# A gated delta-rule layer on one core: taps moved to ScalarE and GpSimd, 2 KB transfer rows, and a new order on every engine

## What is computed

```python
def attn(h):                       # h = layernorm(x)
    q, k, v, z = split(h @ w_qkvz.T)          # 32 heads of 64
    b, a = split(h @ w_ba.T)
    q, k, v = conv4(q), conv4(k), conv4(v)    # causal, 4 taps, each channel by itself
    g, beta = -exp(A_log) * softplus(a + dt_bias), sigmoid(b)
    q, k = l2norm(q) * 64 ** -0.5, l2norm(k)
    for t in range(256):                      # per head
        S = S * exp(g[t])
        S = S + outer(k[t], (v[t] - k[t] @ S) * beta[t])
        o[t] = q[t] @ S
    return rmsnorm(o) * norm_weight * sigmoid(z) @ w_out.T
x = x + layernorm(attn(layernorm(x)))
x = x + layernorm((silu(gate) * up) @ w_down.T)   # gate, up from layernorm(x) @ w_gate_up.T
```

## Time and profile before

| | us |
|---|---|
| median of 3 runs | 3099.59 |
| range of these | 3080.13 to 3100.36 |
| the profiled execution | 3095.35 |
| its span in the trace | 3093.5 |

### The profile page before, as it was taken

How to read it: one execution, slowest core, us unless ns; L and a number is a source line. 1 busy time by engine, 2 the same in 40 slices (tenths; PEclk the granted TensorE clock), 3 DMA queues, 4 the chain that set the end, 5 groups by cost and what they waited for, 6 DMA issues and landing times. The chain is left out here.

```text
span 3093.5 us, 101425 instructions
## 1 busy us (share of the span) xinstructions
PE 2889.1 (93%) x42816; PEld 1953.0 (63%) x42816; DVE 2445.7 (79%) x5610; ACT 1752.3 (57%) x3242; POOL 1103.3 (36%) x904
## 2 busy tenths in 40 slices
PE   6699999999999999999999999999999999789998
PEld 3366666666666666666666666666666666655555
DVE  7688888888888888888888888888888888656554
ACT  6456666566556666666566566656666566424332
POOL 1444344444444444343444444444343344100000
PEclk9899999999999999999999999999999999899999
DMA  5454545554545555554455555544455445300000
GB/s 154 79 82 84 89 80 83 83 98 81 81 81 97 80 81 84 93 83 80 81 98 84 82 80 99 83 76 83 75 100 81 80 81 84 83 21 21 27 14 21
DMA packets 1298099, 241.85 MB, mean 78 GB/s; under 512 B 1248240, under 2 KB 1269104, under 8 KB 1296496
## 3 DMA queue, kind: packets, MB, share of 16 engines
q1 hardware_dynamic: 1297648, 235.36, 44.2%
HBM read 120.13 MB, written 39.58 MB: 52 GB/s over the span
## 5 line engine op out<-in xcount | busy, mean ns | idle before, releaser
L1342 PE MATMUL bank<-xT,w_sb 128*128 128x512 f32 x2048 | 982.1, 613 | 10.0 <-PEq L516 5.2
L784 POOL TENSOR_TENSOR kq<-kq,product 128x510 f32<-128x510 f32 (+2 forms) x384 | 448.9, 1182 | 723.4 <-ACT kq L873 713.4
L1342 PEld LDWEIGHTS bank<-xT,w_sb 128*128 128x128 f32 x2048 | 372.3, 191 | 374.4 <-issue 346.1
L772 POOL TENSOR_TENSOR dec_ap<-gcrow,gcb 128x1024 f32<-128x1024 f32 x64 | 121.8, 1902 | 657.2 <-DMA gcb<-gcb_d 657.2
L1088 DVE SCALAR_TENSOR_TENSOR kq<-bank,cw,kq 128x510 f32<-128x510 f32 (+2 forms) x384 | 285.7, 744 | 58.8 <-ACT kq L873 49.5
L1088 DVE SCALAR_TENSOR_TENSOR v_c<-bank,cw,v_c 128x510 f32<-128x510 f32 (+2 forms) x384 | 285.8, 744 | 15.9 <-ACT v_c L873 6.9
L1353 PE MATMUL bank<-kq 64*64 64x128 f32 x4096 | 276.7, 273 | 20.4 <-POOL kq L784 8.3
L940 ACT COPY delta<-bank 128x256 f32<-128x256 f32 x256 | 95.2, 372 | 341.8 <-PE bank L1410 341.5
L1457 PE MATMUL bank<-wo,u_sq 128*128 128x256 f32 x1024 | 261.0, 399 | 4.0 <-DVE u_sq L1180 3.5
L879 ACT ACTIVATE product<-bank,cw 128x512 f32<-128x512 f32 x384 | 249.1, 684 | 6.8 <-PE bank L1342 2.8
L1435 PE MATMUL bank<-ap_mat,delta 64*64 64x64 f32 x4096 | 243.0, 219 | 3.2 <-issue 3.1
(11 more groups left out here) (168 smaller groups left out, 5459.4 us busy)
## 6 DMA issues: line engine op xcount, KB each, us to landing
xT<-xT_d SPq DMA_DIRECT2D x64, 512.0 KB, 3.9
gcrow<-gcrow_d SPq DMA_DIRECT2D x128, 256.0 KB, 4.6
k_r<-k_tok SPq DMA_DIRECT2D x512, 64.0 KB, 2.3
v_r<-k_tok SPq DMA_DIRECT2D x512, 64.0 KB
a_d<-ap_mat SPq DMA_DIRECT2D x256, 64.0 KB
z_t<-z_d SPq DMA_DIRECT2D x256, 64.0 KB, 2.5
w_sb<-in_w_qkvz SPq DMA_DIRECT2D x8, 1024.0 KB, 6.8
x_un<-eye_un SPq DMA_DIRECT2D x64, 128.0 KB, 4.0
```

The lines of the kernel that those rows point to most:

```text
L784: nc.gpsimd.tensor_tensor(t[:, :, d:SEQ], t[:, :, d:SEQ], prod[:, :, 0:SEQ - d], ALU.add).then_inc(tap_added[i], 1)
L1342: ins = nc.tensor.matmul(bank[:, :], w_two[m.grp % 2][:, h, s * P:(s + 1) * P], xT[:, h, :], start=(h == 0), stop=(h == HT - 1))
```

## The change

It has three parts.

The first: the three further taps of v's second pair of heads (projection 5) become three ScalarE products and three GpSimd sums, as for q. `add_tap(m, 2, d)` adds into v_c. `TAPPED` gives the projection for each of the three.

The second: k_tok, v_r and k_r are laid out by halves of a row. The first half of all 16 groups comes first, then the second half (`by_half`), so a row of a `turned` transfer is 16 x 32 elements in one piece, 2 KB. `turn_v`, `turn_k`, `scale_k`, `scale_v`, `squares`, `residual` and `solve(0)` read or write through this layout.

The third: every engine's list in `turn` has a new order, with other waits and other bank places. The work per step is the same. TensorE's list now handles steps s[0] to s[4].

```diff
+            TAPPED = (2, 3, 5)
+
+            def by_half(t):
+
+                return t[:, :, :].rearrange("p g c -> p (g c)").rearrange("p (f g c) -> p f g c", f=2, c=W2)
+
+            def over_halves(t):
+
+                return t.rearrange("p (o g x) -> p o g x", o=1, x=1).broadcast_to([P, 2, G, W2])
...
-                                    sp.dma_start(dst[r:r + W2, :, W2 * f:W2 * f + W2], k_tok[q:q + W2, :, W2 * t:W2 * t + W2]) \
+                                    sp.dma_start(by_half(dst)[r:r + W2, f, :, :], by_half(k_tok)[q:q + W2, t, :, :]) \
...
-                        t = half_of(m, 1)[:, a, :].rearrange("p (s t) -> p s t", t=SEQ)
+                        t = (half_of(m, 1)[:, a, :] if a < 2 else v_c[:, 1, :]).rearrange("p (s t) -> p s t", t=SEQ)
...
-                        i, w = (TAPS - 1) * a + d - 1, (2 + a) * TAPS + TAPS - 1 - d
+                        i, w = (TAPS - 1) * a + d - 1, TAPPED[a] * TAPS + TAPS - 1 - d
...
-                        ins = nc.vector.transpose(k_tok[:, a * GP:(a + 1) * GP, :].rearrange("p g c -> p (g c)"), v_c[:, a, :])
+                        ins = nc.vector.transpose(by_half(k_tok)[:, :, a * GP:(a + 1) * GP, :], v_c[:, a, :].rearrange("p (g f c) -> p f g c", f=2, c=W2))
...
-                        nc.vector.tensor_tensor(kt[m.par][:, :, :], k_r[:, :, :], col(e_tail).broadcast_to([P, G, C]), ALU.mult).then_inc(kt_done, 1)
+                        nc.vector.tensor_tensor(kt[m.par][:, :, :].rearrange("p g (f c) -> p f g c", f=2), by_half(k_r), over_halves(e_tail), ALU.mult).then_inc(kt_done, 1)
```

SyncE's list, in which the transfers at the end of a turn change places:

```diff
-                            wait_for(sp, zt_done, s[5], 1)
-                            z_out(s[5])
-                            x_out(s[5])
-                            wait_for(sp, z_d_out, s[5], 16)
-                            z_back(s[5])
-                            wait_for(sp, x_d_out, s[5], 16)
-                            x_back(s[5])
-                        if s[3]:
-                            wait_for(sp, proj_full[4], s[3], 1, back=1)
-                            load_x(s[3])
                         if s[4]:
-                            identity_in(s[4])
+                            wait_for(sp, sub_done[14], s[4], 1)
+                            x_out(s[4])
+                            wait_for(sp, zt_done, s[4], 1)
+                            z_out(s[4])
+                            wait_for(sp, z_d_out, s[4], 16)
+                            z_back(s[4])
+                        if s[2]:
+                            wait_for(sp, proj_full[6], s[2], 1, back=1)
+                            load_x(s[2])
+                        if s[3]:
+                            wait_for(sp, x_d_out, s[3], 16, back=1)
+                            identity_in(s[3])
+                        if s[4]:
+                            wait_for(sp, x_d_out, s[4], 16)
+                            x_back(s[4])
```

More of the change, by code:

```diff
@@ new lines, in turn @@
+                        if s[2]:
+                            wait_for(dve, z16_done, s[2], 1)
+                            turn_back(s[2])
+                        if s[1]:
+                            wait_for(dve, tap_added[8], s[1], 1)
+                            turn_v(s[1], 1)
+                        if s[3]:
+                            wait_for(dve, var_log[1], s[3], 1)
+                            combine(s[3], 1, ring(s[3], 2))
+                        if s[1]:
+                            scale_k(s[1])
@@ L1560, in turn @@
-                        if s[3]:
-                            wait_for(pe, zoff_done, s[3], 1)
-                            solve(s[3], 0)
+                        if s[3]:
+                            wait_for(pe, delta_done[0], s[3], 1)
+                            advance(s[3], 0)
+                        if s[1]:
+                            project(s[1], 4, ring(s[1], 1))
+                        if s[3]:
+                            wait_for(pe, og_done[0], s[3], 1, back=1)
+                            output(s[3], 0)
+                            wait_for(pe, state_done[0], s[3], 1)
+                            key_state(s[3], 1)
@@ new lines, in turn @@
+                        if s[4]:
+                            wait_for(pe, z_exp[1], s[4], 1, back=-3)
+                            wait_for(pe, og_done[0], s[4], 1)
+                            project_out(s[4], 1, ring(s[4], 0))
+                        if s[3]:
+                            wait_for(pe, rhs_done[1], s[3], 1)
+                            solve(s[3], 1)
+                        if s[4]:
+                            project_out(s[4], 0, ring(s[4], 2))
+                        if s[3]:
+                            wait_for(pe, delta_done[1], s[3], 1)
+                            advance(s[3], 1)
+                            output(s[3], 1)
+                            wait_for(pe, state_done[1], s[3], 1)
+                            key_state(s[3], 2)
@@ new lines, in turn @@
+                        if s[1]:
+                            wait_for(pe, tap_prod[3], s[1], 1)
+                            project(s[1], 5, ring(s[1], 3))
+                        if s[3]:
+                            wait_for(pe, rhs_done[2], s[3], 1)
+                            solve(s[3], 2)
+                        if s[1]:
+                            wait_for(pe, tap_added[2], s[1], 1)
+                            scores(s[1], 0, ring(s[1], 2))
+                        if s[3]:
+                            wait_for(pe, delta_done[2], s[3], 1)
+                            advance(s[3], 2)
+                            output(s[3], 2)
+                            wait_for(pe, state_done[2], s[3], 1)
+                            key_state(s[3], 3)
@@ new lines, in turn @@
+                        if s[1]:
+                            project(s[1], 6, ring(s[1], 0))
+                        if s[3]:
+                            wait_for(pe, rhs_done[3], s[3], 1)
+                            solve(s[3], 3)
+                        if s[1]:
+                            wait_for(pe, tap_added[5], s[1], 1)
+                            wait_for(pe, tap_prod[8], s[1], 1)
+                            scores(s[1], 2, ring(s[1], 3))
+                        if s[3]:
+                            wait_for(pe, delta_done[3], s[3], 1)
+                            output(s[3], 3)
```

667 lines of the change are left out of this document (308 added, 359 removed).

## The result

The changed kernel took 3065.48 us, median of 7 runs (3060.48 to 3074.76), beside 3087.17 for the kernel before: ratio 0.992 with a 95% interval of 0.989 to 0.995. The forecast was 3034, a gain of 65 us; 22 came. Run twice more, each time on another chip, the same kernel gave 1.000 (0.998 to 1.002) and 1.000 (0.998 to 1.002). So the change is worth between nothing and 22 us.

A forecast was written before the change was run, and what follows sets the result against it. The matrix engine, busy 479.27 of 500 us, was taken as the bound, its idle as all there was to win. Terms -55 - 32 - 7 - 12 + 31 + 10 = -65 gave 3030 us profiled, 3034 beside the median, range 2992 to 3108.

The forecast's parts named there:

- PE's work itself is only put in another order.: Matrix engine, steady part: the reordering leaves its work as is; all the change can win lies in 1.67 us idle per turn.
- Group weights, +10 (0 to 14): Before join16_outer: next group's weights load ahead of identity_in and x_back, delaying x_row up to 2 us, 7 times: +10 us.
- Lower clock, -12: Behind the matrix engine's pauses: half of the 0.4 us per turn lost at 1.2 GHz comes back, -12 us (0 to -25).
- Pauses, -55: Runs of small matmuls: projections put between them let instruction blocks land, cutting 0.98 us idle per turn to 0.1, -55 us.
- the third rival: Matrix engine's pauses aren't the supply of instructions, so 55 and 12 us stay: 3101 us, chance 0.10.
- key_state 1, -32: Before key_state 1: project 4 between advance 0 and output 0 covers the wait for the state copy, 0.52 us per turn.
- z_t, -7: Before join16_inner: projections 5 and 6 ahead give z_t time to land, 0.17 to 0.05 us per turn, -7 us.
- New couplings, +31: Matrix engine's waits for VectorE before project 3, ScalarE before delta_out 0, and residual 1 before solve 1: 0.5 us per turn.
- ScalarE's chain (b): From the end of join_inner to delta_out 0: ScalarE needs 7.3 us against 7.1 of cover, late by 0.2.
- Taps 0, rows 0: VectorE's three fused tap operations saved, and 2 KB instead of 128 B transfer rows for k and v, each counted 0.
- rival 4: Moving the taps does nothing: the 2.2 us of VectorE are counted at zero; part of the forecast, no chance of its own.
- Rival 1: Pauses go but waits come in their place, 0.5 us becoming 1.5 per turn: +62, 3096 us, chance 0.15.

The follow-up runs named there:

- the weights late: Changed kernel with the next group's weights issued behind x_back instead of ahead of x_row and x_back: 3047.02 us (0.9898), then 3052.89 (0.9918) and 3057.20 (0.9933).
- the small program: Separate program without the computation, only large and small matmuls grouped, alternating or alone, with or without transfers: 2.21 us per pair and block grouped, 2.53 alternating.
- the second profile: The changed kernel, unaltered, run again on a second chip: 3076.13 us, ratio 1.0004.
- the later profile of before: The kernel before, unaltered, profiled again on another chip: 3071.96 us, 1.64 us idle a turn.
- the third of the changed kernel: The changed kernel, unaltered, run a third time on another chip: 3080.15 us, ratio 1.0000.
- a split project_out: Changed kernel with two extra 64-row matmuls in the middle of each project_out: 3100.90 us (1.0074); with them ahead of it instead, 3083.61 (1.0014).

## Why the prediction was wrong

The direction of the first comparison was right and its time lies in the range (2992 to 3108), but two thirds of the gain didn't come.

- *"PE's work itself is only put in another order."* This sentence failed. It sets the order's own price at zero; it is 0.67 us a turn, 41 us (0.82 without the 0.15 of wait that the shortest turn of before holds). Three more runs of 128-row matmuls make it, at some 0.3 us each. The trace of before had it already: 5.35 from start to start for three projections in one run, and 1.91 at 1539.80 for one alone.
- *Group weights, +10 (0 to 14).* Mis-sized: some 27 by undoing it. The place was right and even the sign of failure ("seven long waits before join16_outer of more than 2 us"); the waits are 2.6 each, and the clock behind each was not counted.
- *Lower clock, -12.* It gave back nothing: 27 slow projection matmuls before, 24 after (17 against 11 and 14 on other chips), since seven new long waits replaced the pauses as its main cause: of nine places with slow ones in the changed kernel six stand behind them. With the weights late 0 to 4 are left, so the step would have come.
- *Pauses, -55.* Without the seven waits for x_row the issue rows fell from 64 to 13 us, on later chips from 53 to 14: -52 and -39. The mechanism stands: the small program shows pauses at every 256th instruction and none where large matmuls stand between. So the third rival is out. By the Trainium skill (Runtime: NRT & Kernel Launch, "Instruction fetch mechanics") the cost of a block boundary is mostly hidden. In the small program that holds only with 128-row matmuls among the instructions: without them TensorE stops for 0.58 us in the mean.
- *key_state 1, -32.* 31.1 to 0.2 us, on later chips 38.8 to none. Right, and in full.
- *z_t, -7.* 10.5 to 0 and 7.4 to 0. Right.
- *New couplings, +31.* 18 us, on later chips 28: 10 to 11 for conv's result and residuals, and 8 to 17 for the state ahead of key_state 3, which the list of couplings doesn't have, though the new order takes its cover away (20.5 in the second profile). Of ScalarE's chain (b) nothing was seen. The size is near, the places are only in part.
- *Taps 0, rows 0.* The rows are 0. The taps are 0 only in a sum of separate terms: taken back in the new order they cost 40 to 58 us. The order could not stand without them. Whether the move does nothing in the old order, as rival 4 has it, was not tried.
- *Rivals.* Rival 1 came nearest by its time (3096 against 3065 to 3080), but not by its mechanism; VectorE was late for project 3 by 9.4 us in all, not by 149.

In the first pair the terms give: idle (-52 - 31 - 10 + 10 + 8 + 18) = -57, busy time +41 (0.66 a turn), together -16, against -20.6 for the two profiled executions. For the later profile of before and the third of the changed kernel, which are of two chips, idle is -39 - 39 - 7 + 11 + 17 + 17 = -40, and busy time +42 against it is nothing, as the ratio of 1.000.

## What to carry to other kernels

When waits are traded for cover by spreading large matmuls among small ones, count the runs: each separate one costs a fixed time (0.3 us here) on the engine that is the bound, and is worth it only where the hand-over that it covers is longer. Moving a covering block uncovers what it covered; look first for what stood on both sides of it. And see which instruction waits before a line of waits is called a remainder: the wait for the state went from one key_state and came up at another. Check where a rare large transfer stands in its queue: seven of them cost as much here as half the pauses. And a gain under one per cent wants more than one chip before it is believed.

## What the hardware showed that was not expected

- Changing between 64-row and 128-row matmuls costs TensorE some 0.3 us for the two changes of a run: 0.1 going in and 0.2 coming out in the kernels, 0.35 at a split project_out, 0.3 in the small program.
- TensorE stops for 0.25 to 0.94 us at each 256th instruction of small matmuls even with idle DMA engines, and not at all with 1.9 us of large matmuls ahead of each 256. I had taken the pause for 1.2 to 1.6 us.
- A bare wait can cost more than itself: behind 1.28 us of wait in a turn the granted clock was 0.50 for 5 us, three projections taking 8.14 in place of 5.42 us.

```profile
1179.00:1184.00 5.00, 5.00 (x19) 2.35 (x16) 4.76 (x12) 3.04 (x6) 1.90 (x1) 0.50 0.65 88
```

- The same pair of kernels gave ratios whose intervals don't meet (0.989 to 0.995, then twice 0.998 to 1.002), each time on another chip, with the shortest turn of each kernel the same in every profile of the table.
